# Attention scores over 8 and 9 rows of a head in place of 32, in a four-layer Flamingo block on one core

## What is computed

```
x = x + tanh(g_xattn[0]) * xattn0(layernorm(x), ctx)   # 16 heads of 8, Wq Wk Wv Wo with biases
x = x + tanh(g_ffn[0])   * moe(layernorm(x))           # rms norm, 16 experts, top 4, x + mixture
x = x + tanh(g_xattn[1]) * xattn1(layernorm(x), ctx)   # one head of 128
x = x + tanh(g_ffn[1])   * ffn1(layernorm(x))          # 128 -> 512, two butterflies, gelu, -> 128
xattn0: softmax(q k^T / sqrt(8)) v per head, then Wo, bo
```

## Time and profile before

| | us |
|---|---|
| median of 3 runs | 442.6 (442.52 to 453.13) |
| profiled execution | 445.5 |
| its span | 443.7 |
| TensorE busy | 379.1 |
| VectorE busy | 266.6 |
| ScalarE busy | 198.5 |
| POOL busy | 217.8 |

### The profile page before, as it was taken

One profiled execution on the slowest core, in us unless ns is written; L12 is line 12 of the kernel. 1 busy time (PEld: TensorE's weight loads), 2 busy tenths in 40 slices (PEclk: granted clock), 3 DMA queues, 4 the chain that ended last, 5 costly groups with the idle time before them and its releaser, 6 DMA issues.

```text
span 443.7 us, 7130 instructions
## 1 busy us (share of the span) xinstructions
PE 379.1 (85%) x2654; PEld 246.4 (56%) x2654; DVE 266.6 (60%) x690; ACT 198.5 (45%) x372; POOL 217.8 (49%) x205
## 2 busy tenths in 40 slices
PE   5477679768978897999999999999999999578774
PEld 3244567556766674565555555555555565235554
DVE  8561566886668615856567857677666735552501
ACT  2142035533435434556545475464744457135222
POOL 6589899889794310744445424453343533400000
PEclk9696758985769657999999999999999999978999
DMA  8754333735441100000000000000000000000001
GB/s 254 116 109 114 95 118 125 129 108 141 107 133 49 52 0 1 1 1 1 0 0 1 1 1 1 0 0 2 0 0 0 2 0 0 1 0 1 24 25 47
DMA packets 7425, 19.55 MB, mean 44 GB/s; under 512 B 1208, under 2 KB 2396, under 8 KB 7264
## 3 DMA queue, kind: packets, MB, share of 16 engines
q0 software_dynamic: 3168, 11.54, 8.8%
q1 hardware_dynamic: 3504, 6.56, 6.7%
q10 hardware_dynamic: 720, 1.01, 0.7%
HBM read 16.02 MB, written 1.05 MB: 38 GB/s over the span
## 4 chain that ended last, share of the span: by engine, by line
PE 68%; DVE 13%; ACT 6%; DMA 6%; issue 3%; SPq 3%; POOL 1%; ACTq 0%; DVEq 0%
PE bank L843 12%; PE bank L710 7%; PE bank L828 6%; PE bank L829 6%; PE bank L830 6%; PE bank L835 5%; PE bank L736 5%; PE bank L952 4%; PE bank L963 3%; DMA rings<-qt_row 3%; DMA rows<-in_rows 3%; PE bank L717 2%; DVE nt L1078 2%; DVE pick_e L1072 2%; SPq L238 2%
## 5 line engine op out<-in xcount | busy, mean ns | idle before, releaser
L1279 DVE SCALAR_TENSOR_TENSOR rings<-rings,bank 128x512 f32<-128x512 f32 x64 | 43.9, 685 | 69.3 <-ACT rings L573 57.0
L400 POOL TENSOR_TENSOR rings<-rings 128x512 f32<-128x512 f32 x32 | 41.1, 1284 | 78.4 <-DVE rings L1282 69.9
L573 ACT ACTIVATE rings<-bank,b1c 128x512 f32<-128x512 f32 x64 | 44.1, 689 | 77.8 <-PE bank L830 77.4
L828 PE MATMUL bank<-xhl,w_hi 128*128 128x512 f32 x128 | 75.9, 593 | 0.0
L400 POOL TENSOR_TENSOR wide<-rings 128x512 f32<-128x512 f32 x32 | 41.8, 1306 | 47.5 <-DVE rings L1282 33.8
L1078 DVE TENSOR_REDUCE nt<-bank 128x4 f32<-128x480 f32 x64 | 40.0, 650 | 30.9 <-PE bank L717 30.9
L710 PE MATMUL bank<-rings,ks 32*120 32x128 f32 x512 | 49.0, 344 | 6.6 <-DVE nt L1078 5.1
L717 PE MATMUL bank<-ks,rings 32*128 32x120 f32 x512 | 47.6, 337 | 4.2 <-ACT qt_row L454 2.9
L829 PE MATMUL bank<-xhl,w_lo 128*128 128x512 f32 x128 | 51.1, 399 | 0.0
L830 PE MATMUL bank<-xhl,w_hi 128*128 128x512 f32 x128 | 51.0, 399 | 0.0
L710 PEld LDWEIGHTS bank<-rings,ks 32*120 32x120 f32 x512 | 41.7, 235 | 13.5 <-issue 11.0
(11 more groups left out here) (188 smaller groups left out, 684.6 us busy)
## 6 DMA issues: line engine op xcount, KB each, us to landing
bw<-in_flies POOLq DMA_DIRECT2D x18, 512.0 KB, 4.1
bw<-in_L_ffn_w POOLq DMA_DIRECT2D x4, 512.0 KB, 4.7
x_sb<-in_x SPq DMA_DIRECT2D x4, 256.0 KB, 7.7
rings<-qt_row SPq DMA_DIRECT2D x16, 64.0 KB
x_sb<-in_L_ffn_w SPq DMA_DIRECT2D x1, 1024.0 KB, 4.9
out<-xr SPq DMA_DIRECT2D x4, 256.0 KB, 2.4
wide<-in_ctx ACTq DMA_DIRECT2D x4, 240.0 KB, 7.9
ks<-kt_row SPq DMA_DIRECT2D x16, 60.0 KB
```

Of the source, the lines that this page charges most:

```text
L400: pool.tensor_tensor(es[e % len(es)], eq[:, e % 2, :], ec[:, e % 2, :], ALU.mult).then_inc(s["m_s"], 1)
L573: act.activation(esg[:, e % 2, :], SB[1 + e % 2][:, :], ACT.Gelu_apprx_sigmoid, bias=b1c[:, 0, e:e + 1]).then_inc(s["m_sg"], 1)
L828: pe.matmul(bk[:, :], w1_hi[:, e, branch, :], low(g), start=True, stop=False)
L1279: dve.scalar_tensor_tensor(eq[:, j, :], esg[:, j, :], GELU_LIMIT, (PQ, PO)[j][:, :], ALU.min, ALU.mult).then_inc(s["m_eq"], 1)
```

## The change

The maxima no longer go through VectorE. ScalarE copies the transposed maxima (16 rows) to `mxr`, and SP sends them by one DMA per sequence into row 8 of each 32 of `qs`. The matmuls for the maxima read 8 rows, the turned ones 9 (L710, L717). `qm`, the zero rows and their fills go. `kt_row` and the queries get four buffers. The first norm runs over 4 and then 12 sequences. ScalarE copies the values; the bias of the first attention's values goes through Wo into the row bias, that of the second is added later by POOL. `pick_e` is written once by ScalarE at the start; POOL takes the row biases; SP's loads are reordered; the router of group 0 runs a turn earlier; the norm's statistics go by halves of 8 sequences; four (`LATE`) of POOL's 18 butterfly stages and the up bias's last two go into pass 0 of the experts. Names, semaphores and counts that only follow are left out below.

```diff
-            for g in range(2, G):
-                sp.wait_ge(s["kt_rdy"], g + 1)
-                sp.wait_ge(s["qt_rdy"], g + 1)
-                sp.wait_ge(s["st_mm"], (g - 1) * GB * HG)
-                stack_k(g)
-                stack_q(g)
-            sp.wait_ge(s["xr_rdy"], G)
-            sp.dma_start(w2_sb[:, :, :], a["L0_ffn_w2"]).then_inc(s["ld_w2"], 16)
+            sp.wait_ge(s["qt_rdy"], 1)
+            stack_q(0)
+            sp.wait_ge(s["kt_rdy"], 2)
+            stack_k(1)
+            sp.wait_ge(s["qt_rdy"], 2)
+            stack_q(1)
+
+            def stack_max(b):
+                sp.wait_ge(s["mxr_rdy"], b + 1)
+                sp.dma_start(qs[HD:P:32, (b // GB) % 2, :, b % GB * P:(b % GB + 1) * P], mxr[:, b % 2, :]
+                             ).then_inc(s[f"mx_ld{b % 2}"], 16)
+
+            for b in range(NB):
+                stack_max(b)
+                g = b // GB + 1
+                if b == 2:
+                    sp.wait_ge(s["xr_rdy"], G)
+                    sp.dma_start(w2_sb[:, :, :], a["L0_ffn_w2"]).then_inc(s["ld_w2"], 16)
+                if b % GB == 0 and 2 <= g < G:
+                    sp.wait_ge(s["kt_rdy"], g + 1)
+                    sp.wait_ge(s["st_mm"], (g - 1) * GB * HG)
+                    stack_k(g)
+                if b % GB == 1 and 2 <= g < G:
+                    sp.wait_ge(s["qt_rdy"], g + 1)
+                    stack_q(g)
...
-            pool.memset(qs[:, :, :, :], 0.0).then_inc(s["qs_zero"], 1)
-            own.mark(pool.memset(nt[:, :, :], 0.0))
-            own.then_wait(pool.memset(vst[:, :, :, :], 0.0))
+            own.mark(pool.memset(vst[:, :, :, :], 0.0))
+            own.wait()
...
-            inverse_root(1, NB, False)
-            for g in range(G):
-                pool.wait_ge(s[f"ld_x{g}"], 16)
+            inverse_root(1, GB, False)
+            pool.wait_ge(s["ld_kb"], 16)
+            pool.tensor_copy(bvb[:, :], bcol[:, CV0:CV0 + 1].to_broadcast([P, P])).then_inc(s["bvb_rdy"], 1)
+            inverse_root(2, NB - GB, False)
             fetch(0)
             fetch(1)
...
+            pool.tensor_scalar(b1c[:, :], b1_in[:, 1, :], 1.0, None, ALU.add).then_inc(s["b1_rdy"], 1)
...
+            pool.wait_ge(s["bo_rdy"], 1)
+            for g in range(G):
+                rows_ = slice(g * GB, (g + 1) * GB)
+                pool.tensor_tensor(xr[:, rows_, :], x_sb[:, rows_, :],
+                                   bcast[:, BO, :].unsqueeze(1).to_broadcast([P, GB, D]), ALU.add).then_inc(s["xr_rdy"], 1)
+            own.then_wait(pool.tensor_tensor(bcd[:, :], bcast[:, BC, :], bcast[:, BD, :], ALU.add))
+            own.then_wait(pool.tensor_scalar(bcd[:, :], bcd[:, :], tg[:, 3:4], None, ALU.mult))
...
+            def values1(g):
+
+                seqs = slice(g * GB, (g + 1) * GB)
+                pool.wait_ge(s["v_rdy"], 2 * G)
+                pool.tensor_tensor(v1_all[:, seqs, :], v1_all[:, seqs, :],
+                                   bcast[0:M, BV1, :].unsqueeze(1).to_broadcast([M, GB, D]), ALU.add).then_inc(s["v1_rdy"], 1)
...
+            for k in range(2 * STAGES - LATE):
+                for op in range(3):
+                    stage(k, op)
+                if k == STAGES:
+                    inverse_root(3, HALF, True)
...
                     product(g, e)
-                    if e == LAG - 1 and first(g):
-                        inverse_root(3, GB, True)
+                    if first(g) and e < 3 * LATE:
+                        stage(2 * STAGES - LATE + e // 3, e % 3)
+                    if first(g) and e == 3 * LATE:
+                        pool.tensor_copy(bft[0:1, 0:1], bfly[0:1, STAGES % 2, 0:1]).then_inc(s["bf_rdy"], 1)
+                        pool.wait_ge(s["bf_rdy"], 1)
+                        up_bias_stages()
+                    if first(g) and e >= 3 * LATE:
+                        values1(e - 3 * LATE)
+                    if e == E - 2 and first(g):
+                        inverse_root(4, HALF, True)
                     if e == LAG + 2 and not first(g):
-                        inverse_root(g + 3, GB, False)
+                        inverse_root(g + 4, GB, False)
...
+            def both_values(g):
+                for half in range(2):
+                    b = g * GB + 2 * half
+                    act.wait_ge(s["v_mm"], 2 * g + half + 1)
+                    act.activation(v_all[:, b:b + 2, :], bank[6 + half][0:M, :].rearrange("p (u d) -> p u d", u=2),
+                                   ACT.Copy).then_inc(s["v_rdy"], 1)
...
-                if g >= 2:
-                    act.wait_ge(s[f"qs_ld{g % 2}"], 16 * HG)
-                act.activation(qt_row[:, g % 2, :], bank[0][:, :], ACT.Identity,
+                act.activation(q_rows[g], bank[2][:, :], ACT.Identity,
                                bias=bcol[:, CQ0:CQ0 + 1]).then_inc(s["qt_rdy"], 1)
 
+            act.wait_ge(s["which_rdy"], 1)
+            act.activation(pick_e[:, :, :], which2[:, :].unsqueeze(2).to_broadcast([32, E, P]), ACT.Copy
+                           ).then_inc(s["pick_rdy"], 1)
...
+            def turned_max(b):
+                act.wait_ge(s["nt_turned"], b + 1)
+                need(act, f"mx_ld{b % 2}", 16 * (b // 2))
+                act.activation(mxr[:, b % 2, :], TP[0:HG * HR, 0:P], ACT.Copy).then_inc(s["mxr_rdy"], 1)
...
+            turned_max(0)
             spread_values(0)
             for b in range(NB + 2):
+                if b + 1 < NB:
+                    turned_max(b + 1)
                 if b < NB:
                     exps(b, 0)
                     exps(b, 1)
                 if 0 <= b - 1 < NB:
                     heads_out(b - 1)
-                if b == NB - 1:
+                if b == NB - 2:
                     normed_t(0)
+                if b == NB + 1:
+                    gates_t(0)
                 if 0 <= b - 2:
...
             turn_rows0(0)
+            keys(2)
             pe.wait_ge(s["ld_wb"], 16)
             queries(0)
             turn_rows0(1)
+            both_values(2)
             queries(1)
-            keys(2)
+            keys(3)
             turn_rows0(2)
-            both_values(2)
-            queries(2)
-            turn_rows0(3)
-            pe.wait_ge(s["us_rdy"], 1)
-            pe.matmul(bank[1][:, 0:HC], ubs[:, 1, :], ident[0:HC, 0:HC], start=True, stop=True).then_inc(s["ub_turned"], 1)
-            queries(3)
-            pe.wait_ge(s["qt_rdy"], G)
-            pe.wait_ge(s["xnt_rdy"], G)
-            pe.wait_ge(s["ub_rdy"], 1)
...
-                            mm = pe.matmul(turned_bank(b, gg)[0:M, r * P:(r + 1) * P], ks[32 * gg:32 * gg + 32, i, r, mc],
-                                           qm[32 * gg:32 * gg + 32, b % 2, r, :], start=True, stop=True)
+                            mm = pe.matmul(turned_bank(b, gg)[0:M, r * P:(r + 1) * P], ks[32 * gg:32 * gg + HD + 1, i, r, mc],
+                                           qs[32 * gg:32 * gg + HD + 1, i, r, tc], start=True, stop=True)
                             if r == HR - 1:
                                 mm.then_inc(s["st_mm"], 1)
                         if ahead < NB:
                             n = 2 * half + j
-                            rows32 = slice(32 * OF[n], 32 * OF[n] + 32)
-                            mm = pe.matmul(score_bank(ahead, n)[:, r * M:(r + 1) * M], qs[rows32, ia, r, ta],
-                                           ks[rows32, ia, r, ma], start=True, stop=True)
+                            rows8 = slice(32 * OF[n], 32 * OF[n] + HD)
+                            mm = pe.matmul(score_bank(ahead, n)[:, r * M:(r + 1) * M], qs[rows8, ia, r, ta],
+                                           ks[rows8, ia, r, ma], start=True, stop=True)
                             if r == HR - 1:
...
-                pe.transpose(TP[:, 0:P], nt[:, :, :].rearrange("p g c -> p (g c)"), ident[:, :]).then_inc(s["nt_turned"], 1)
+                pe.transpose(TP[0:HG * HR, 0:P], nt[:, b % 2, :, :].rearrange("p g c -> p (g c)"), ident[:, :]).then_inc(s["nt_turned"], 1)
...
             phase(-2, 0)
-            keys(3)
+            queries(2)
+            both_values(3)
+            turn_rows0(3)
+            queries(3)
+            pe.wait_ge(s["k1_rdy"], G)
+            pe.wait_ge(s["bvb_rdy"], 1)
+            pe.matmul(bank[5][:, 0:P], bvb[:, :], wt[:, WO0, :], start=True, stop=True).then_inc(s["bo_mm"], 1)
+            pe.wait_ge(s["qt_rdy"], G)
             phase(-2, 1)
-            both_values(3)
             phase(-1, 0)
             pe.wait_ge(s["v_rdy"], 2 * G)
             turn_max(0)
             phase(-1, 1)
             pe.wait_ge(s["kt_rdy"], G)
-            pe.wait_ge(s["k1_rdy"], G)
+            pe.wait_ge(s["bo_rdy"], 1)
             for b in range(NB):
                 phase(b, 0)
                 if b + 1 < NB:
                     turn_max(b + 1)
                 if b >= 1:
                     values(b - 1)
+                if b == NB - 1:
+                    pe.wait_ge(s["ld_moe"], 16 * 2)
```

(64 more changed lines are left out.)

213 lines of the change are left out of this document (85 added, 128 removed).

## The result

The kernel after takes 470.4 us (median of four runs, 468.78 to 471.38), the kernel before 442.6 us beside it: ratio 1.066, interval 1.058 to 1.074. It is slower by 28 us where I had forecast 26 us faster. Executions of one kernel differ by some per cent, the longer ones at a lower granted clock: medians here are over all executions, ratios and their intervals over the shorter ones alone, and the profiles of b_shallow, a_scores32, a_late0 and a_split are of longer ones. The profiled execution took 469.4 us with a span of 467.2 us, 23.5 us more than before's 443.7 us.

What follows compares the result with a forecast made beforehand. TensorE was taken to bound the kernel, its clock switching between full and half in the attention loop. The profiled span of 443.7 - 7 - 16 - 4 + 1 = 417.7, 26 us less, gave 416 us from the median, range 403 to 437.

Steps and rivals of the forecast that it cites:

- The loop: Attention loop, values of sequence 0 to 15: three sequences at half clock, twelve at full, 88 us against 104, gain 16.
- the round trip: Per sequence in the loop, maxima copied and transferred: 3.5 us, showing 0.2 to 0.4 us at full clock, none at half.
- rival 2: Attention loop: shallow scores leave the clock low for all 15 sequences, 124 us for 104, total 455 us; chance 0.11.
- Start: Up to the values of sequence 0: earlier norm and buffers bring them at 53.7 against 60.84 us, gain 7 us.
- Handover: From the values of sequence 15 to the first gate product: 8 us in place of 12.1, gain 4 us.
- First pass: Experts' first pass: POOL's four late butterfly stages just fit beside its products; loss 1 us, range 0 to 4.
- Rival 1: Attention loop: the new maxima transfer needs 5 us and sets the pace, 7.0 us a sequence, total 433 us; chance 0.10.
- Rival 3: Experts' first pass: POOL late, down products waiting for it, 4 us or more, total 421 to 425 us; chance 0.08.

Runs made afterwards that it cites:

- b_shallow: The kernel before with only its score matmuls cut to 8 rows and its turned scores to 12: 469.0 us, ratio 1.054.
- a_scores32: The kernel after with only the scores over 32 rows, the turned scores staying at 9: 454.3 us, ratio 1.032.
- a_late0: a_deep with the four late butterfly stages moved from the first expert pass back into the attention loop's time: 442.8 us, ratio 1.002.
- a_split: a_deep without late stages, root and refinement back at experts 2 and 4, and the experts' first norm spread over three sequences: 436.8 us, ratio 0.992.
- a_deep: The kernel after with both groups of attention matmuls reading 32 rows again, the added rows zeros: 451.2 us, ratio 1.025.
- a_16: The kernel after with both groups of attention matmuls over 16 rows, the added rows zeros: 468.2 us, ratio 1.063.
- a_24: The kernel after with both groups of attention matmuls over 24 rows, the added rows zeros: 454.8 us, ratio 1.031.
- a_place: a_deep with late stages kept, only the second half's root moved to expert 2 and its refinement to expert 4 of the first pass: 446.9 us, ratio 1.016.

## Why the prediction was wrong

**The loop: the step that failed.** I wrote "The clock is low at the start (before until 69 us) and I take three sequences of it". All fifteen were low. Everything about the work itself in that part held: the steps at full clock take 4.9 us in a_deep (5.1 forecast), at half clock 7.8 us (8.2), matmuls 8 rows deep keep their length at a given clock (270 ns at full, 416 at half in the median, 32 rows deep too), and the round trip hides at half clock and shows little at full. The forecast rested on the clock alone, and there the argument against rival 2 was the error: "from 66 to 90 us ... it stayed at 0.92 or above although TensorE idled 3.7 of 24 us, so the loop has something to spare". It has something to spare in time, as the deep loops show, but I read that as room in depth. a_16 gives back none of it; a_24 reaches a mean clock of 0.69 where a_deep reaches 0.80. The earlier trace rows held the hint, TensorE 15.99 of 17 us busy at 0.50 with two row groups in place of four, and I gave it 0.11. The 8.2 us itself was read from a row that does not fit: the 8.27 us of the earlier trace rows are for 73 matmuls, not for "the same", and the 9.56 us hold 1.6 us of idle; the first row there has 103 matmuls in 7.22 us at 0.50.

The Trainium skill (TensorE: Matmul & The Clock Gate, Part 1) lets the clock follow how busy TensorE is. By the loop of the kernel after this is not enough: 116 of 120 us busy, all at 0.50, with no wait over 2.7 us. The measurement decides, and depth counts.

**Rival 2** is what happened, with its mechanism and nearly its size: 124 us for the loop against 120.3 measured. Its sum of +13 us missed 470.4 by 15, because it took over the two steps below from the forecast, and because the last stage had 5.3 us of low clock that no run ties to the change. Its loop and handover were too dear by 6 us, and of the 15 some 4 lie between profiles and medians: the profiled execution of before was 3 us above its median, after's 1 us below.

**Start.** Right: 7 us forecast, 6.4 measured. First rows at 15.65 us (16.3), scores at 30.4 (29.5), turned scores at 45.9 (45.5), values at 54.4 (53.7). In the timeline of VectorE no wait for the `rows` transfer is left:

```profile
15.65 1.11 DVE L1092 TENSOR_SCALAR rings<-x_sb,mean,rr 128x128 f32<-128x128 f32 x4
```

**Handover.** 4 us forecast, 3.2 measured, although the clock was low until 181.8 us; the gain of 1 us that rival 2 left was too low.

**First pass.** "It just fits ... Loss 1 us; 0 to 4" was mis-sized: 5.3 us, taken back whole by LATE = 0. The sum of 8.6 us of GpSimd in 8.7 had counted the instructions but not their place: a product behind a stage is late even if the total fits. In that pass VectorE's products waited 3.8 us in all for GpSimd, and TensorE's gate products 3.2 us for VectorE. Of the 5.3 us some 2.8 were lost in the gate steps at experts 9 and 10, within the late stages, and 2.5 in those at experts 13 and 14, where TensorE also waited 1.5 us for the end of the butterfly before it turned its rows.

**Second pass.** Missing from the sum. I had priced the root of 16 values among GpSimd's work at experts 12 to 15, and left out what is queued behind it: the product of expert 15, VectorE behind that product, and the refinement, which VectorE did in the first pass before the change. It cost 6.6 us, 6.3 of them in the one gate step of 10.4 us, a wait of 4.6 us and the low clock behind it.

**Rival 1** did not come: the transfer is in the fast steps of 4.9 us without a wait, and costs 5.5 to 8.4 us of waits over the whole loop of a deep kernel. **Rival 3** came in its price, 5.3 us for the 4 it named, but not by its sign: TensorE's down products show no wait for GpSimd in the first pass and one of 0.4 us in the second. The gate products, behind VectorE, did the waiting.

## What to carry to other kernels

Before rows are taken out of a matmul, look at whether its stage lives on TensorE's clock: here rows of zeros cost no time and were worth 19 us (470.4 against 451.2), and the reading is the granted clock beside a busy engine. When work is moved to an engine "that has room", write out the order of its queue at that place and follow what waits for the next item; the total of busy time against the span of the stage hides it. And undo a compound change part by part: its start, its handover and its transfer of the maxima were sound, and with depth, stages and root put back it is 1.3% faster than before (0.3 to 2.3%).

## What was not expected of the hardware

With TensorE busy 97% of 120 us the granted clock stayed at 0.50 for matmuls 8, 9, 12 and 16 rows deep in four row groups, came back in part at 24 rows (0.69 over the loop) and more at 32 (0.80), and the added rows held only zeros. Value matmuls 120 rows deep stood between them in every case. A VectorE product of 16 elements a partition took up to 4.95 us beside GpSimd (in a_place), against 0.17 us alone.
